# Second pass of an AdaLN, mLSTM and mixture-of-experts kernel: wide filler products, one score block moved, the b2 sums and their split moved

## What is computed

```python
h = layernorm(x) * (1 + ca) + sa                 # ca, sa, ga, cb, sb, gb come from silu(c) @ wmod, one set per row
x = x + ga * mlstm(h)                            # 512 steps of a gated recurrence, d_head = 64
h = layernorm(x) * (1 + cb) + sb
logits = h @ Wr + br                             # 8 experts, the best 2, softmax over those two -> gate
y = einsum('te,eth->th', gate, relu(h @ W1 + b1) @ W2 + b2)
x = x + gb * y                                   # W1: 8 x 128 x 256, W2: 8 x 256 x 128
```

## Time and profile before

| what | value |
|---|---|
| median of 3 runs (lowest, highest) | 347.52 us (343.4, 347.57) |
| the profiled execution's own time | 346.4 us |
| its span, first to last instruction | 344.4 us |
| busy in the span: PE, PEld, DVE, ACT, POOL | 321.0, 258.9, 277.4, 164.3, 176.5 us |
| mean granted TensorE clock | 0.975 of 2.4 GHz |
| chain that ended last, by engine | PE 80%, DVE 7%, DMA 3%, ACT 3%, POOL 3%, issue 2% |

### The profile page before, as it was taken

One profiled execution on the slowest core, in us unless ns is written; L12 is line 12 of the kernel. 1 busy time (PEld: TensorE's weight loads), 2 busy tenths in 40 slices (PEclk: granted clock), 3 DMA queues, 4 the chain that ended last, 5 costly groups with the idle time before them and its releaser, 6 DMA issues.

```text
span 344.4 us, 4964 instructions
## 1 busy us (share of the span) xinstructions
PE 321.0 (93%) x1700; PEld 258.9 (75%) x1700; DVE 277.4 (81%) x794; ACT 164.3 (48%) x300; POOL 176.5 (51%) x177
## 2 busy tenths in 40 slices
PE   2989997999999999999999999999999999878995
PEld 1969884888687868887788868786878688656883
DVE  5586678489879996999699978998779968784774
ACT  1452525165454737555546453654556363434442
POOL 7720460158554873487438852686408740684340
PEclk9999988599999999999999999999999999998999
DMA  5760005100071005200340016000610061006101
GB/s 132 237 193 0 2 0 206 42 2 0 4 244 30 3 0 206 71 0 1 109 169 2 0 35 245 0 0 4 244 33 0 0 228 49 1 1 220 58 0 30
DMA packets 13726, 24.13 MB, mean 70 GB/s; under 512 B 1779, under 2 KB 8102, under 8 KB 12678
## 3 DMA queue, kind: packets, MB, share of 16 engines
q1 hardware_dynamic: 13474, 23.70, 20.9%
q10 hardware_dynamic: 164, 0.07, 0.1%
q0 software_dynamic: 64, 0.07, 0.1%
HBM read 21.60 MB, written 2.23 MB: 69 GB/s over the span
## 4 chain that ended last, share of the span: by engine, by line
PE 80%; DVE 7%; DMA 3%; ACT 3%; POOL 3%; issue 2%; SPq 1%; DVEq 0%; POOLq 0%
PE bank L1023 10%; PE bank L1024 8%; PE bank L1025 8%; PE bank L1035 8%; PE bank L1045 8%; PE bank L1036 8%; PE bank L978 6%; PE bank L963 3%; PE bank L911 3%; PE bank L1068 2%; PE bank L1062 2%; DMA br_bc<-in_L_ffn_br_dram 2%; PE bank L926 2%; PE bank L931 1%; PE bank L1054 1%
## 5 line engine op out<-in xcount | busy, mean ns | idle before, releaser
L447 POOL TENSOR_TENSOR hg_lo<-hg,hg_hi 128x512 fp32r<-128x512 f32 x69 | 92.6, 1352 | 70.2 <-ACT hg_hi L501 70.2
L806 DVE SCALAR_TENSOR_TENSOR hg<-bank,neg_b,gate_bc 128x512 f32<-128x512 f32 x128 | 94.3, 741 | 30.8 <-DMA gate_bc<-gates_d 15.4
L501 ACT ACTIVATE hg_hi<-hg 128x512 fp32r<-128x512 f32 x128 | 79.8, 628 | 79.0 <-DVE hg L806 77.7
L1023 PE MATMUL bank<-h_hi,w_hi 128*128 128x512 f32 x128 | 58.9, 460 | 2.3 <-ACT gate_rows L539 2.3
L1025 PE MATMUL bank<-h_lo,w_hi 128*128 128x512 f32 x128 | 51.6, 403 | 0.0
L1035 PE MATMUL bank<-hg_hi,w_hi 128*128 128x512 f32 x128 | 51.6, 403 | 0.0
L1024 PE MATMUL bank<-h_hi,w_lo 128*128 128x512 f32 x128 | 51.6, 403 | 0.0
L1045 PE MATMUL bank<-hg_lo,w_hi 128*128 128x512 f32 x128 | 51.0, 399 | 0.0
L1036 PE MATMUL bank<-hg_hi,w_lo 128*128 128x512 f32 x128 | 50.7, 396 | 0.0
L416 POOL TENSOR_SCALAR var_eps<-mv 128x4 f32<-128x4 f32 x16 | 4.9, 304 | 76.8 <-DVE mv L573 76.8
L818 DVE TENSOR_TENSOR hg_lo<-hg,hg_hi 128x512 fp32r<-128x512 f32 x59 | 42.8, 725 | 0.5
(11 more groups left out here) (160 smaller groups left out, 547.4 us busy)
## 6 DMA issues: line engine op xcount, KB each, us to landing
gate_bc<-gates_d SPq DMA_DIRECT2D x8, 1024.0 KB, 7.0
gate_bc<-gates_d SPq DMA_DIRECT2D x16, 256.0 KB, 3.6
gate_bc<-gates_d SPq DMA_DIRECT2D x8, 512.0 KB, 5.0
out_dram<-x_all SPq DMA_DIRECT2D x8, 256.0 KB, 2.3
w_raw<-in_L_ffn_W_dram SPq DMA_DIRECT2D x1, 1024.0 KB, 8.9
x_all<-in_L_attn_x_dram SPq DMA_DIRECT2D x2, 256.0 KB, 4.1
wmod_sb<-in_L_wmod_dram SPq DMA_DIRECT2D x1, 384.0 KB, 4.8
gates_d<-gate_rows SPq DMA_DIRECT2D x8, 16.0 KB
```

The costliest lines, as they stand in the source:

```text
L447: g.tensor_tensor(hg_lo[k][:, :], hg[k][:, :], hg_hi[k][:, :].bitcast(fp32), ALU.subtract).then_inc(s_lo_pool, 1)
L501: a.activation(hg_hi[k][:, :], hg[k][:, :], ACT.Copy).then_inc(s_hghi, 1)
L806: v.scalar_tensor_tensor(hg[k][:, :], up_bank[n % 4][:, :], neg_b1[:, n:n + 1], gate_bc[own % 2][:, n // NU, :], ALU.max, ALU.mult).then_i ...
L1023: t_.matmul(dst, w_hi, hx, start=True, stop=False)
```

## The change

`keep_busy_wide(n)` is a new function: n fp32 products of the identity with 512 columns of `w1_raw`, into the whole of bank 3. In the second pass the narrow fillers (two per step) stay in steps 4 to 7. Steps 8 to 12 get one wide product each in their place, and step 13 gets two wide ones in place of four narrow ones, ahead of the wait for the gates. Step 8 waits first for the load of W1. Score block 2 moves behind up product 1 (step 17). `b2_parts` is cut in two: the three additions run on VectorE at the end of step 6, clearing, copies and subtraction at the end of step 10. ScalarE's `gateT` moves from step 15 to step 16, behind the weights of blocks 3 and 2.

```diff
+    WIDE_FILL = {8: 1, 9: 1, 10: 1, 11: 1, 12: 1, 13: 2}
...
-                    if t == N - 1 and end:
+                    if t == (N if opening else N - 1) and end:
                         act.wait_ge(s_grow, m1 + 1)
                         a.activation(row2(gateT, m1)[0:LO2 + E, :], gate_rows[:, :], ACT.Copy).then_inc(s_ghi, 1)
...
-            def b2_parts():
+            def b2_sums():
                 dve.wait_ge(s_b2w, 1)
                 dve.wait_ge(s_b2, 48)
                 for o in (0, LO, LO2):
                     last = v.tensor_tensor(b2_raw[o:o + E, :], b2_raw[o:o + E, :], y_bank[o:o + E, 0:D], ALU.add)
                 last.then_inc(s_b2s, 1)
+
+            def b2_split():
                 v.memset(b2_parts3[:, :].bitcast(fp32), 0.0).then_inc(s_b2z, 1)
...
-                    if opening and t == 13:
-                        b2_parts()
+                    if opening and t == 6:
+                        b2_sums()
+                    if opening and t == 10:
+                        b2_split()
...
+            def keep_busy_wide(n):
+                for _ in range(n):
+                    t_.matmul(bank[3][:, :], ident[:, :], w1_raw[:, 0:2, :].rearrange("p e f -> p (e f)"), start=True, stop=True)
...
-                    if first and t > LAG or opening and LAG < t < N - 3:
+                    if first and t > LAG or opening and LAG < t < 8:
                         keep_busy(2)
+                    if opening and t == 8:
+                        pe.wait_ge(s_w1, 16)
+                    if opening and t != 13:
+                        keep_busy_wide(WIDE_FILL.get(t, 0))
...
                         if opening:
-                            keep_busy(4)
+                            keep_busy_wide(WIDE_FILL[t])
                         pe.wait_ge(s_gates, b + 2)
...
-                    chain(b, end, start, t)
+                    if not (opening and t == N):
+                        chain(b, end, start, t)
+                    if opening and t == N + 1:
+                        chain(b, end, start, N)
```

More of the change, by code:

```diff
@@ L482, in weights, with body @@
                 last.then_inc(s_E, 1)
-            def body(b, end, start, ahead, live, weights_hi=False):
+            def body(b, end, start, ahead, live, weights_hi=False, opening=False):
                 m1, m2 = b + 1, b + 2
@@ L555, in _ @@
             body(-2, False, True, True, lambda n: False, weights_hi=True)
-            body(-1, True, True, True, lambda n: n >= N)
+            body(-1, True, True, True, lambda n: n >= N, opening=True)
             for b in range(B - 3):
```

## The result

The changed kernel takes 342.02 us in the median of 19 runs (340.5 to 344.93), the kernel before 346.7 us in as many (342.85 to 350.15). The ratio is 0.991, 95% interval 0.988 to 0.994; it leaves out executions over 1.5% above the fastest of their kernel, four of the kernel before, and so lies nearer to 1 than the ratio of the two medians, 0.987. That is faster by about 1%, inside the 2% that counts as no clear difference here. On another chip the same pair gave 0.987, 0.983 to 0.991 (experiment 12). The profiled execution took 341.54 us, span 339.6.

The account below looks back on a forecast made before the run. TensorE (PE) was taken to bound the steady passes. 1.64 idle + 5.1 clock - 0.5 gates - 0.6 stall = 5.6 us off the profiled 346.4 gave 340.8, shifted 0.2 to 341.0; range 338.8 to 345.0.

Parts of the forecast that it names:

- The clock: Second pass: if TensorE stays at 2.4 GHz, the 10.20 us become 5.10, so 5.1 us saved.
- the long slow stretch: TensorE at 1.2 GHz from 58.2 to 68.4 us in the kernel before, PE busy for all 10.20 us.
- The chance of 0.66: Chance given to case A, the forecast of 341.0 us.
- case B: Rival: the clock falls all the same, around gates and L963 or behind score block 2; about 344 us, chance 0.29.
- 1.64 us of idle time: TensorE's wait before score block 2 was to shrink from 2.09 to 0.45 us.
- d: Lateness reaching the gates from the b2 split in step 10; bounds 0 and 1.25 us, taken 0.5.
- 51.15 + d: Forecast start of the gates' transposes on TensorE, in us; 51.32 in the kernel before.
- Rival C: Slower: wide products themselves run at 1.2 GHz, the clock having fallen when step 8 begins; 352 us, chance 0.05.
- the paragraph on steps 12 and 13: Wide fillers there cost nothing if the clock stays up; at 1.2 GHz they end 1.2 us after the transposes began.
- Late next: After the score multiplications: hg bound by the gates' first piece, and TensorE stalling for VectorE's hh 0.4 to 0.9, taken 0.6.
- case A: The forecast: the clock holds through the second pass and into the third; 341.0 us, chance 0.66.
- late slow stretch: TensorE at 1.2 GHz from 310.8 to 314.1, 3.3 us at half; its absence worth 1.7, giving 339.

Follow-up runs that it names:

- experiment 12: The changed kernel again, without an edit, on another chip: ratio 0.987 to the kernel before, median 342.43 us.
- experiment 5: The kernel before with only score block 2 moved behind up product 1 and gateT behind the weights: ratio 0.986, median 342.66 us.
- experiment 4: The changed kernel with b2's clearing, copies and subtraction moved from step 10 to step 13, between maximum and mask: ratio 0.985 to the kernel before, median 340.95 us.
- experiment 11: The kernel before with the new order (score block 2, gateT) and wide fillers, b2 block whole in step 13: ratio 0.986, median 341.65 us.

## Why the prediction was right, and where it was not

**The clock.** Right in kind: the long slow stretch is gone from the profiled execution, and that is most of the gain. The size was not: 5.1 us came from halving 10.20, and 4.41 were saved. The prediction's own row had an expert matmul at 0.43 and at 0.24, which is more than half; by that ratio the 10.20 us save 4.5. The chance of 0.66 was for the result and not for a share of executions, so the executions are no test of it: of the 25 of the changed kernel, 16 have a mean clock of 0.99 or more (340.5 to 343.7 us), three 0.987 and six 0.982 (344.2 to 344.9, case B's 344).

**Score block 2.** Idle 0.45 forecast, 0.25 measured, so 1.84 was saved and not 1.64. That the order alone carries most of the gain I did not see: I counted it into 1.64 us of idle time, together with the b2 move. Experiment 5 shows it shortens the slow stretch as well.

**d.** The size was nearly right, the working was not. "Bounds 0 and 1.25, taken 0.5" was meant for the gates, and they are 0.61 late; but I let h_lo alone stand before the copies, so the logits' addition had an upper end of 1.23 and was 1.82 late. That only 0.61 of it reached the gates is partly luck: VectorE no longer stood behind GpSimd at L747, which the working had, nor at `top_d`, which it had not. Behind h_lo, one copy got through and the next instruction of GpSimd was served before the third. The rule of the Trainium skill (SBUF — State Buffer, Who interferes with whom) that whoever issues first holds the port for its whole instruction agrees with the trace, for copies as well: 1.09, 0.22 and 0.98 beside GpSimd, 0.22 each without it (experiment 4).

**What waits for `a_col`.** Missed. Its subtraction stands behind the logits' addition on VectorE, so TensorE waited 1.24 us in step 12, all of step 13 slid, and the fillers there, which I had at nothing, ended 0.56 behind the gates. So the transposes, which were to start at 51.15 + d, started 1.12 behind 51.15. That is a wide product on the path even at 2.4 GHz; at 1.2 GHz it is experiment 12, where the transposes came 2.65 later than before (7.95 behind the logits, 5.30 before). Rival C's price for these steps was 2.8; the 1.2 in the paragraph on steps 12 and 13, which had no wait for `a_col`, was too little. It is rival C in a small form, inside case B.

**Late next.** Right in kind: hg waits for the first piece of the gates (0.60), which was issued 0.95 later (0.3 forecast) and landed 3.24 behind its issue (3.6 forecast). L910 stalls for hh: 0.20 idle, and it starts 0.38 later behind the transposes of `h_ga` than L904 did, against 0.4 to 0.9 forecast and 0.6 taken.

**The sum.** Up to L910 it can be redone from the rows: 1.84 + 4.41 - 0.61 - 0.38 = 5.26, and L910 does start 5.26 ahead of L904 (63.94 and 69.20). Forecast was 5.6, so the terms were the right ones, and the one most off, the clock at 5.1, was partly made up for by the idle time and the stall. From profiled execution to profiled execution 4.9 is left: the steady passes give back 0.7, for which no experiment was made, and the end brings 0.3. The 1.7 that case A counted for an absent late slow stretch is not there: the stretch is absent, and the span is no shorter for it than by these 0.3. Against the medians, 341.0 was 6.5 below the 347.52 of three executions; over 19 the kernel before has 346.7, and the changed one, at 342.02, is 4.7 below that.

## What to carry to other kernels

The same instructions have different prices at different places: before a step moves, look who shares a port with it there, and what stands behind it on its own engine. When several edits aim at one gap, run each alone: here one reordering, free of cost, gave in the median what the whole change gave. A filler ahead of a wait is free only while the clock and the thing waited for are on time.

## What the runs showed of the hardware

Three fp32 copies on 8 partitions, 128 columns each, took 0.68 us with GpSimd idle and 2.31 beside two of its 512-column instructions; a clearing of 128 x 128 at 46.09 took its usual 0.17 beside h_lo. Executions of one kernel differ by up to 4.4 us, in part with the granted clock: 340.5 us at a mean of 0.999, 344.9 at 0.982. Not all of it is the clock: of the 3.4 us between the two profiled executions of the changed kernel, 1.15 lie ahead of the second pass's logits, where the clock was 1.00 in both. And the same wait of 1.40 us before score block 2 was followed by a fall in experiment 5 and by none in experiment 11, the same wait of 1.24 for `a_col` by a fall in experiment 12 and by none in the profiled execution above: the rows don't say what decides.
